# Two-layer block: second attention layer's scores in f32 lanes of 32 rows, without split, stores and stack, and its last batch done tile by tile

## The reference

```python
# layer 0: attention with 32 heads of 8 over 8 key groups, softmax over 256 keys, no mask
# layer 0 ffn: product-key experts
h = silu(xn @ W_up.T + b_up) @ W_down.T + b_down          # 1024 wide, then 128
scores, idx = top_k(sim(q(h), keys), 8)                   # 8 heads, 2 x 45 keys
sc, pk = top_k(all 64 sums, 8)                            # 8 of 2048 experts per token and head
z = silu((h . down_embed[indices]) * softmax(sc)); out = sum z * up_embed[indices]
# layer 1: attention with 16 heads of 16 over 4 key groups, causal, ALiBi bias slope[head] * (k - q)
scores = einsum('brgtd,bgsd->brgts', qg, k) / 4 + bias;  softmax over k <= q
# layer 1 ffn: x rounded to int8 per token, product with int8 weights, scaled, f16
```

## Time and profile before

| what | value |
|---|---|
| median of 3 runs | 785.51 us (784.35 to 786.27) |
| the profiled execution: its own time, its span | 787.66 us, 785.8 us |
| busy: PE, DVE, ACT, POOL | 528.0, 592.4, 255.8, 514.9 us |
| instructions | 9193 |
| DMA packets, bytes | 47765, 125.49 MB |
| first and last gather issued | 38.15 us, 703.23 us |
| mean granted PE clock (share of 2.4 GHz) | 0.823 |

### The profile page before, as it was taken

The page is one execution under the profiler, slowest core; times in us unless marked ns, Lnnn a source line. Parts: engine busy times, 40 slices in busy tenths (PEclk is TensorE's granted clock), DMA queues, the critical chain, the costliest instruction groups (busy, mean ns, idle before and its releaser), DMA issues.

```text
span 785.8 us, 9193 instructions
## 1 busy us (share of the span) xinstructions
PE 528.0 (67%) x2241; PEld 291.8 (37%) x2258; DVE 592.4 (75%) x2700; ACT 255.8 (33%) x648; POOL 514.9 (66%) x522
## 2 busy tenths in 40 slices
PE   2810466486794567797758558956356996979786
...
GB/s 292 38 165 220 168 173 155 154 156 155 151 223 162 156 156 165 232 153 153 210 198 159 156 158 160 158 237 186 210 191 153 154 153 256 157 142 1 106 2 15
DMA packets 47765, 125.49 MB, mean 160 GB/s; under 512 B 10715, under 2 KB 20507, under 8 KB 46654
## 3 DMA queue, kind: packets, MB, share of 16 engines
...
q10 hardware_dynamic: 600, 0.30, 0.2%
...
## 4 chain that ended last, share of the span: by engine, by line
POOL 50%; issue 18%; PE 13%; DVE 12%; DMA 5%; ACT 1%; POOLq 0%; ACTq 0%; DVEq 0%
POOL rows L551 50%; DMA rows<-experts_table,idx 5%; PE experts L831 3%; DVE hot L1204 3%; DVE acc L1229 2%; PE outs L777 1%; PE experts L839 1%; PE turn L586 1%; PE turn L811 1%; DVE nmax L1245 1%; DVE nmax L1237 1%; PE scores L743 1%; DVE bestp L1129 1%; DVE var L1072 1%; PE turn L807 1%
## 5 line engine op out<-in xcount | busy, mean ns | idle before, releaser
L551 POOL DMA_INDIRECT rows<-experts_table,idx x512 | 505.0, 986 | 188.7 <-issue 151.4
L1204 DVE CUSTOM_DVE_ANT_0 hot<-rows,h 128x128 f32<-128x128 f32 x512 | 114.6, 287 | 108.6 <-DMA rows<-experts_table,idx 108.4
L831 PE MATMUL experts<-rows,diag 128*128 128x256 f32 x384 | 132.4, 497 | 45.4 <-ACT diag L1049 38.2
L683 PE MATMUL turn<-stackk,stackq 125*128 125x256 bf16 x256 | 58.4, 344 | 105.8 <-DVE nmax L1237 52.1
L1229 DVE SCALAR_TENSOR_TENSOR acc<-rows,zs,acc 128x256 f32<-128x256 f32 x304 | 125.7, 478 | 0.9 <-issue 0.3
L831 PEld LDWEIGHTS experts<-rows,diag 128*128 128x128 f32 x384 | 93.3, 254 | 76.5 <-ACT diag L1049 47.0
L997 ACT ACTIVATE probs<-scores 128x512 f32<-128x512 f32 x176 | 97.3, 594 | 59.6 <-PE scores L734 31.1
L1043 ACT ACTIVATE zt<-za 128x8 f32<-128x8 f32 x64 | 13.4, 209 | 259.5 <-DVE za L1208 259.3
L1049 ACT ACTIVATE diag<-ident,zs 128x128 f32<-128x128 f32 x192 | 63.1, 394 | 68.3 <-DVE zs L1214 63.8
L1237 DVE TENSOR_REDUCE nmax<-turn 128x2 f32<-128x512 f32 x128 | 82.2, 682 | 1.8 <-PE turn L683 1.7
L683 PEld LDWEIGHTS turn<-stackk,stackq 125*128 125x128 bf16 x256 | 21.7, 111 | 143.8 <-DVE nmax L1237 78.5
...
## 6 DMA issues: line engine op xcount, KB each, us to landing
rows<-experts_table,idx POOLq DMA_INDIRECT x512, 3.2
...
```

The lines of the kernel that those rows point to most:

```text
L551: nc.gpsimd.indirect_dma_start(rows[:, slot, c, :], None, tab, bass.IndirectOffsetOnAxis(ap=idx[:, b % 2, t, TOP * h + c:TOP * h + c + 1], ...
L683: ins = mm(ps[:, t * S:(t + 1) * S], stackq[0][r, m, t * P:(t + 1) * P], stackk[0][r, m // QUAD, :], start=True, stop=True)
L831: ins = mm(experts[:, s // FH, :], diag[:, g % 2, k, :], rows[:, g % RING, k, PRIV:ROW], start=(s % FH == 0 and k == 0), stop=(s % FH == F ...
L1204: ins = v.tensor_tensor_reduce(out=zjunk[:, k, :], in0=rows[:, slot, k, 0:PRIV], in1=h2[:, b % 2, t, :], scale=1.0, scalar=0.0, op0=ALU.mu ...
```

## The change

- **Second layer's scores** are f32 products from SBUF, on *lanes*: q1 and k1 hold each key group's 16 dimensions in 32 partitions of its own (rows 2 to 17), with row 1 for the slope (q1: slope, k1: position) and row 0 for the maximum (k1: ones). `qkv1` writes them directly from padded weights, with three PSUM banks a batch instead of two, and ACT copies once. Gone for this layer are the split, the two stores, the six stack loads, `slopeq`, `slopek`, and the maxima's three parts with their DMA.
- **Maxima** go to `nwide`, which PE transposes in f32 (`nm1`, four a tile), and DVE adds them to q1 (`lift1`), one tile at a time.
- **Last batch tile by tile**: `norm1`, `qkv1`, `round1`, `turnq`, `quant`, `out1`, `flip1`, `proj1`, `fin1` and the output are called once a tile for batch 3; `ctx1`, `nm1` and `lift1` for every batch. Tile 0's maxima, scores and products no longer need tile 1.
- **`warm` is gone.**
- **Start**: GpSimd clears v0, v1 and `nwide` first and waits for the first normalisation before it clears the stacks; `ones` waits for that; ACT's conversions (`init` 1 and 2), which wait for weights, stand later.
- **New orders** of all four plans. Second layer's `max1` of batches 0 to 2 now lies earlier among `sc0` of the next batch, and the second layer of batch 2 ends before `add` 63.

The diff, cut to its core (the rest are the same functions with a tile argument, the other parts of the plans, and names without an index for the layer):

```diff
+LANE, SLOPE, FIRST = 32, 1, 2
...
-WARM = (28, 8, 14)
...
+    nm1:2.1 quant:2.0 flip0:3.0 sc1:2.4 sc1:2.5 sc1:2.6 proj0:3.0 pv1:2.2 sc1:2.7 sc1:2.8 ctx1:2.0 sc1:2.9 add:0.61 pv1:2.3
+    pv1:2.4 sc1:2.10 sc1:2.11 norm1:3.0 pv1:2.5 qkv1:3.0 qkv1:3.1 add:0.62 ctx1:2.1 max1:3.0 max1:3.1 max1:3.2 add:0.63 max1:3.3
+    flip1:2.0 nm1:3.0 proj1:2.0 sc1:3.0 sc1:3.1 sc1:3.2 sc1:3.3 norm1:3.1 pv1:3.0 pv1:3.1 qkv1:3.2 qkv1:3.3 turnq:3.0 ctx1:3.0
+    max1:3.4 max1:3.5 max1:3.6 max1:3.7 max1:3.8 max1:3.9 max1:3.10 max1:3.11 quant:3.0 flip1:3.0 turnq:3.1 nm1:3.1 quant:3.1
+    proj1:3.0 sc1:3.4 sc1:3.5 sc1:3.6 sc1:3.7 pv1:3.2 sc1:3.8 pv1:3.3 sc1:3.9 sc1:3.10 sc1:3.11 pv1:3.4 pv1:3.5 ctx1:3.1
+    flip1:3.1 proj1:3.1
 """
...
+    init:0.0 norm0:0.0 up:0.0 up:0.1 init:0.1 up:0.2 up:0.3 fold:0.0 init:0.2 down:0.0 sim:0.0 texp:0.2 qkv0:0.0 keep:0.0
...
+    over0:3.1 lift1:2.1 dots:0.61 out1:2.0 zs:0.61 acc:0.61 res0:3.0 over1:2.0 norm1:3.0 dots:0.62 zs:0.62 acc:0.62 dots:0.63
+    max1:3.0 max1:3.1 zs:0.63 over1:2.1 acc:0.63 max1:3.2 mix:3.1 max1:3.3 res0:3.1 lift1:3.0 norm1:3.1 fin1:2.0 round1:3.0
+    round1:3.1 over1:3.0 max1:3.4 max1:3.5 max1:3.6 max1:3.7 max1:3.8 max1:3.9 max1:3.10 max1:3.11 nm1:3.0 out1:3.0 lift1:3.1
+    out1:3.1 fin1:3.0 over1:3.1 fin1:3.1
 """
...
+    x:0.0 weights:0.0 weights:0.1 weights:0.2 weights:0.3 x:1.0 ones:0.0 res:0.0 store0:0.0 stack0:0.0 x:2.0 x:3.0 store0:1.0
+    stack0:1.0 res:1.0 store0:2.0 stack0:2.0 res:2.0 out:0.0 store0:3.0 stack0:3.0 res:3.0 out:1.0 out:2.0 out:3.0 out:3.1
...
+def tiles_of(b, n):
+
+    return slice(0, TT) if b < B - 1 else slice(n, n + 1)
...
+        nwide = sb("nwide", [P, TT, QUAD, P])
+        nlanes = nwide[:, :, :, :].rearrange("p t j (u r) -> p t j u r", r=LANE)
+        nmaxd = sb("nmaxd", [P, QUAD, KV1])
...
-            nc.gpsimd.memset(stackk[0][CLEARED_FROM:P, :, :], 0.0)
-            nc.gpsimd.memset(stackq[0][CLEARED_FROM:P, :, :], 0.0).then_inc(cleared, 1)
-            pool.wait_ge(cleared, 1)
             nc.gpsimd.memset(full(v0), 0.0)
             nc.gpsimd.memset(full(v1), 0.0).then_inc(cleared, 1)
+            pool.wait_ge(cleared, 1)
+            nc.gpsimd.memset(v0one, 1.0)
+            nc.gpsimd.memset(v1one, 1.0)
+            nc.gpsimd.memset(full(nwide), 0.0).then_inc(cleared, 1)
             pool.wait_ge(cleared, 2)
-            nc.gpsimd.memset(v0one, 1.0)
-            nc.gpsimd.memset(v1one, 1.0).then_inc(cleared, 1)
+            pool.wait_ge(xn0_ready, 1)
+            nc.gpsimd.memset(stackk[CLEARED_FROM:P, :, :], 0.0)
...
+            def qkv1(b, n):
+                if b == 0 and n == 0:
+                whole = b < B - 1
+                call, part = (0, n) if whole else (n // 2, n % 2)
+                at = columns_of(b, call)
+                pe.wait_ge(drained["norm1"], b + call + 1)
+                ps = bank("qkv1", 3 * b + n)
+                if part == 0:
+                    mm(ps[:, at], full(rowk), posk[:, at], start=True, stop=False)
+                    for c in range(DC):
+                        mm(ps[:, at], wk1[:, c, :], x1T[:, c, at], start=False, stop=(c == DC - 1))
+                    ins = values_of(ps, wv1, x1T, None, tiles_of(b, call))
+                else:
+                    each = S if whole else P
+                    for a in range(2 if whole else QUAD):
+                        for c in range(DC):
+                            ins = mm(ps[:, a * each:(a + 1) * each], wq1[:, c, 2 * (part - 1) + a, :], x1T[:, c, at],
+                                     start=(c == 0), stop=(c == DC - 1))
+                ins.then_inc(filled["qkv1"], 1)
...
             def max1(b, m):
-                if m == 0:
+                u, tq, tk = quad_of(m)
+                if m in (0, QUADS[1]):
                     if b == 0:
-                        pe.wait_ge(late_in, LATE_IN)
                         pe.wait_ge(halves, 2)
-                    pe.wait_ge(stack_in[1], STACK_IN[1] * (b + 1))
-                u, tq, tk = quad_of(m)
+                    pe.wait_ge(drained["qkv1"], projections(b, tq))
                 ps, q, k = bank("max1", UNITS[1] * b + m), slice(tq * P, (tq + 1) * P), slice(tk * P, (tk + 1) * P)
-                each = ps[:, :].rearrange("p (j k) -> p j k", k=P)
-                mm(each, slopek[:, 0, q], slopeq[:, QUAD * u:QUAD * (u + 1), k], start=True, stop=False)
+                near = tq == tk
+                if near:
+                    mm(ps[:, :].rearrange("p (j k) -> p j k", k=P), full(identb),
+                       maskb[:, :].unsqueeze(1).broadcast_to([P, QUAD, P]), start=True, stop=False)
                 for j in range(QUAD):
-                    ins = mm(ps[:, j * P:(j + 1) * P], stackq[1][:, QUAD * u + j, q], stackk[1][:, u, k], start=False,
-                             stop=tq != tk and j == QUAD - 1)
-                if tq == tk:
-                    ins = mm(each, full(identb), maskb[:, :].unsqueeze(1).broadcast_to([P, QUAD, P]), start=False, stop=True)
+                    ins = mm(ps[:, j * P:(j + 1) * P], q1[lane(u), j, q], k1[lane(u), k], start=not near,
+                             stop=not near or j == QUAD - 1)
                 ins.then_inc(filled["max1"], 1)
 
...
+            def nm1(b, t):
+                if t == 0:
+                    pe.wait_ge(drained["max1"], UNITS[1] * b + QUADS[1])
+                else:
+                    pe.wait_ge(nmax1_ready, b + 1)
+                ps = bank("nm1", TT * b + t)
+                for j in range(QUAD):
+                    ins = tr(ps[:, j * P:(j + 1) * P], nwide[:, t, j, :], full(ident))
+                ins.then_inc(filled["nm1"], 1)
...
             def sc1(b, m):
-                if m == 0:
-                    pe.wait_ge(nmax_in[1], 16 * (b + 1))
                 u, tq, tk = quad_of(m)
-                q, k, hd = slice(tq * P, (tq + 1) * P), slice(tk * P, (tk + 1) * P), slice(QUAD * u, QUAD * (u + 1))
+                if m in (0, QUADS[1]):
+                    pe.wait_ge(drained["nm1"], TT * b + tq + 1)
+                q, k = slice(tq * P, (tq + 1) * P), slice(tk * P, (tk + 1) * P)
                 to = scores[:, score_bank(1, UNITS[1] * b + m), :].rearrange("p (j q) -> p j q", q=P)
-                mm(to, slopek[:, 1, k], slopeq[:, hd, q], start=True, stop=False)
-                ins = mm(to, stackk[1][:, u, k], stackq[1][:, hd, q], start=False, stop=tq != tk)
-                if tq == tk:
-                    ins = mm(to, full(identb), maskT[:, :].unsqueeze(1).broadcast_to([P, QUAD, P]), start=False, stop=True)
-                ins.then_inc(scores_ready[1], 1)
+                near = tq == tk
+                if near:
+                    mm(to, full(identb), maskT[:, :].unsqueeze(1).broadcast_to([P, QUAD, P]), start=True, stop=False)
+                mm(to, k1[lane(u), k], q1[lane(u), :, q], start=not near, stop=True).then_inc(scores_ready[1], 1)
...
+            def qkv1(b, n):
+                ps = bank("qkv1", 3 * b + n)
+                whole = b < B - 1
+                call, part = (0, n) if whole else (n // 2, n % 2)
+                at = columns_of(b, call)
+                if part == 0:
+                    wait_from(act, scores_ready[1], UNITS[1] * b)
+                    wait_from(act, pv_done[1], PRODUCTS[1] * b)
+                    fn(k1[:, at], ps[:, at], ACT.Copy)
+                    each = ps[:, S:S + TT * VD].rearrange("p (t g d) -> p t g d", t=TT, d=HD1)
+                    ins = fn(v1at[:, tiles_of(b, call)], each[:, tiles_of(b, call)], ACT.Copy)
+                else:
+                    if b == 0:
+                        act.wait_ge(late_in, LATE_IN)
+                    each = S if whole else P
+                    for a in range(2 if whole else QUAD):
+                        j = 2 * (part - 1) + a
+                        ins = fn(q1[:, j, at], ps[:, a * each:(a + 1) * each], ACT.Identity, bias=slopes[:, j:j + 1], scale=HD1 ** -0.5)
+                ins.then_inc(drained["qkv1"], 1)
 
...
+            def lift1(b, t):
+                dve.wait_ge(filled["nm1"], TT * b + t + 1)
+                dve.wait_ge(filled["max1"], UNITS[1] * b + (QUADS[1] if t == 0 else UNITS[1]))
+                ps = turn[turns.bank["nm1", TT * b + t]]
+                to = q1[:, :, t * P:(t + 1) * P]
+                v.tensor_tensor(to, to, ps[:, :].rearrange("p (j q) -> p j q", q=P), ALU.add).then_inc(drained["nm1"], 1)
...
+    def lanes(m):
+        wide = np.zeros(m.shape[:-1] + (m.shape[-1] // VD, KV1, LANE), m.dtype)
+        wide[..., FIRST:FIRST + HD1] = m.reshape(m.shape[:-1] + (m.shape[-1] // VD, KV1, HD1))
+        return wide.reshape(m.shape[:-1] + (m.shape[-1] // VD, P))
+    wts["wq1"] = lanes(rows_first(a["L1_attn_Wq"]))
+    wts["wk1"] = lanes(rows_first(a["L1_attn_Wkv"][:, :VD]))[:, :, 0]
     wts["wv1"] = rows_first(a["L1_attn_Wkv"][:, VD:])
...
+    slopes = np.zeros((KV1, LANE, QUAD), np.float32)
+    slopes[:, SLOPE] = np.array([start ** (h + 1) for h in range(H1)], np.float32).reshape(QUAD, KV1).T
```

(22 more changed lines are left out.)

680 lines of the change are left out of this document (309 added, 371 removed).

## The result

The changed kernel took 784.71 us (median of 14 executions, 774.05 to 802.77), the kernel before 785.74 beside it (783.71 to 788.89). So it is at most 1% faster, where 3.4% was forecast. The profiled execution, which the rest reads, is the fastest of the 14: 774.05 us, with a span of 772.2. What is read from it explains its own span, shorter by 13.6 us, and not why the median of the 14 is 10.7 us longer.

The account below looks back on a forecast made before the run. It took GpSimd's stream of 512 row gathers, between a head and a tail, to bound the kernel. Head -5.1, stream -1.4 and tail -20.2 sum to -26.7 us, so 785.5 - 26.7 = 759 us; range 745 to 775.

Parts of the forecast that it names:

- Head: Start to first gather (0 to 38.15 us): stack memsets moved behind the first normalisation, -5.1 us, ends -5.6 and 0.
- Stream: GpSimd's row gathers, 38.15 to 706.3 us: -5.4 for a stall gone, +4 for new PE work, together -1.4 us.
- +4 for PE's new work: In the stream: three stretches without slack, where new PE work counts in part against lighter DVE; ends -2 and +13 us.
- Rival B: Stream: PE becomes its holder where scores and maxima of two batches lie together; 786 us and more, chance of slower 0.06.
- Tail: Last rows' arrival to the end: 59.3 us instead of 79.5, -20.2; lower end 50, upper end 72.
- The starting point: Tail: its sum counted from the last rows' arrival as 0, beginning with DVE's `dots`, 2.1 us.
- rival E: Head not shortened, and batch 2's second layer unfinished at the last rows, so PE starts the tail 12 us late: 776, chance 0.06.
- The clock: Tail without `warm`: two stretches at half clock, some 3.5 us lost each, half of it on the path: +3.5 us.
- rival C: Tail runs at half clock without `warm`: tail 72 us, time 772, or 775 with some PE stalls; chance 0.18.
- My own sign of being wrong: Tail: the forecast is wrong if its clock is at half for more than 10 us.
- The price of a lane: Tail, full clock: 0.86 us per 512-column f32 score product, 0.22 per mask, 0.88 per maximum unit, 1.10 with mask.
- changes of shape: Tail: first bf16 product after the ones takes 0.32 instead of 0.22, ten more such changes on the path: 1.0 us.

Follow-up runs that it names:

- bf16_lanes_b: The changed kernel with q1 and k1 of the second layer in bf16, accuracy left out: 744.11 us, 0.9456 of the kernel before.
- pairs_b: The changed kernel with the second layer's maximum and score units of two lanes issued together, in turn, into two banks: 763.88 us, 0.9705 of the kernel before.
- warm_back_c: The changed kernel with 12 unread bf16 filler products, 7 ahead of `max1:3.2` and 5 ahead of `max1:3.4`: 785.17 us, 0.9934 of the kernel before.
- best_warm: best_b with unread bf16 filler products in seven places of the tail where TensorE waited: 751.03 us, 0.9533 of the kernel before.
- best_b: pairs_b with a new order of its tail (`zs` and `acc` 63 ahead of the maxima, tile 1's projections among tile 0's scores): 764.64 us, 0.9681 of the kernel before.
- head_only_b: The kernel before with the changed kernel's start alone: 782.80 us against 786.76, ratio 0.9948.

## Why the prediction was wrong

- **Head, right.** -5.65 for -5.1. PE's first transpose waits for the load of `bup`, which ACT got at 8.35, as foreseen (8.16 before).
- **Stream, right in sign, too cautious.** -5.6 for -1.4. PE's waits vanished from the gathers' row (forecast -5.4), and of the +4 for PE's new work at most the 1.8 us of waits for `acc` were paid there. Rival B did not come to pass in the stream. But the work was paid, in the tail.
- **Tail, wrong: 77.15 for 59.3.** This is the step that failed, and three terms of its sum with it.
  1. *The starting point, +8.8.* The sum began with `dots` 63 at the arrival of its rows. It began 8.8 us later, because PE was still in batch 2's second layer. That was the second half of rival E, which I gave 12 us (with the order and the unit prices of the kernel before, 0.66 and 0.44) and a chance of 0.06, on the ground that "PE is free for over a third of the stream". E's 776 lies near the time measured by luck: its other half, a head that isn't shortened, did not come. PE is free over the stream and full in the last 60 us of it, since +13.5 us a batch (measured: 53.7 us more busy time in all, though 50 fillers went) lands between the last `sc0` and the next batch. bf16_lanes_b and pairs_b show it: less PE work with DVE's order as it was, and the lag is gone (5.03 and 4.86 us from the last issue to `za` 63).
  2. *The clock, 10.0 us for 3.5.* L726 in 2.00 for 1.08, L860 in 2.43 for 1.30, and so on from 712 to 723, from 741 to 751 and at the end. That is rival C's cause; it came together with E's second half, and I had priced each alone. My own sign of being wrong, more than 10 us of the tail at half clock, was there with some 25. I had tied the falls to gaps of PE, and they came without one too (warm_back_c). With the gaps filled and the lanes in pairs, the clock stayed at 1.00 until 745 (best_warm, which ends at 748.9).
  3. *The price of a lane, +1.9.* A score product took 1.05 for 0.86, and a mask behind a lane 0.32 for 0.22; the second was foreseen, in the 1.0 us for changes of shape. A maximum unit without a mask was right (0.84 for 0.88), one with a mask took 0.32 + 1.08 for 1.10. So 10 x 0.19 for the masked and the single score units, less 0.66 for the one pair that overlapped, and for tile 1's maxima 4 x 0.20 less 4 x 0.04.
  The three make 17.2 of the 17.85. They are read from one trace, of the fastest execution. The experiments bear out the first (bf16_lanes_b, pairs_b); for the second they show that filling PE's waits removes the half clock of best_b's tail, not that of the changed kernel's; the split to the microsecond is worked out, not tested.
- **The rule I weighed too low.** Lanes side by side, when issued in turn, were worth some 14 us (777.7 to 763.9); I had given the pairs that happen to stand together 1.7 us and left them to the range. In the two traces 8.8 us of the gain are the lag of the last group. The Trainium skill (TensorEngine Tiling, section "Tiling Modes") has different row tiles load and multiply in parallel; the runs agree for two (105.8 against 59.0 us). The Trainium skill (TensorE: Matmul & The Clock Gate, section "Part 3: Packing small matmuls — row/col tiling") adds that a weight load overlaps with products under way only if its row group differs. The lone lane's 1.05 for 0.86 fits it, but the 0.86 is itself worked out from products of the full array, so no run here shows that the load is the reason.
- **The spread** of the changed kernel, on which the prediction is silent, may have the same root: where PE is full, a stretch at half clock has no slack to vanish in. For it speak the lower mean clock of the longer executions and warm_back_c, with 0.66 in 690 to 700 and a last group 8.4 us later. Against it, head_only_b spreads by 9.7 us with PE busy for 46 of the 60 us from 633. It is argued, not shown: only one of the 14 has a trace.
